# C spread over the partitions by transposes of its columns, and a new order of a chunk's work, in a Mamba and feed-forward block on one core

## The reference

```
xz = x W_xproj^T                 # 96 numbers per token: 64 rank, 16 B, 16 C
dt = softplus(rank W_dt^T + b)   # per token and channel
h  = exp(dt A) h + dt B x        # per channel and state, from token to token
y  = sum over states of h C, plus Dp x
x  = layernorm(x + y)
x  = layernorm(x + (silu(x Wg^T) * (x Wu^T)) Wd^T)
```

## Time and profile before

| | |
|---|---|
| median of 3 runs | 2120.16 us |
| the profiled execution | 2119.75 us |
| its span | 2118.0 us |
| busy: VectorE | 1985.9 us (94%) |
| busy: GpSimd | 1926.8 us (91%) |
| busy: TensorE, matmuls | 1558.5 us (74%) |
| busy: ScalarE | 1303.6 us (62%) |
| mean granted TensorE clock | 0.928 |

### The profile page before, as it was taken

One profiled execution on the slowest core, in us unless ns is written; L12 is line 12 of the kernel. 1 busy time (PEld: TensorE's weight loads), 2 busy tenths in 40 slices (PEclk: granted clock), 3 DMA queues, 4 the chain that ended last, 5 costly groups with the idle time before them and its releaser, 6 DMA issues.

```text
span 2118.0 us, 30230 instructions
## 1 busy us (share of the span) xinstructions
PE 1558.5 (74%) x8621; PEld 1140.7 (54%) x8744; DVE 1985.9 (94%) x2443; ACT 1303.6 (62%) x2157; POOL 1926.8 (91%) x877
## 2 busy tenths in 40 slices
PE   4677778777778777777777777777777877777775
PEld 1545555455555555555555555555555555555553
DVE  5799999999999999999999999999999999999982
ACT  4566666566666656666666666656666656666442
POOL 6999999999999999999999999999999999999950
PEclk6789999999999999999999999999999999999997
DMA  6332433223433322443322443422443422343200
GB/s 219 111 119 86 141 118 137 102 91 112 140 135 120 117 83 104 140 140 115 125 90 89 140 140 115 140 90 76 138 140 115 140 92 86 126 140 107 79 11 20
DMA packets 93455, 239.90 MB, mean 113 GB/s; under 512 B 8593, under 2 KB 42994, under 8 KB 77042
## 3 DMA queue, kind: packets, MB, share of 16 engines
q1 hardware_dynamic: 93426, 239.55, 32.5%
HBM read 220.65 MB, written 18.87 MB: 113 GB/s over the span
## 4 chain that ended last, share of the span: by engine, by line
issue 30%; POOL 28%; DVE 26%; PE 8%; ACT 6%; DVEq 2%; POOLq 1%; another core or an unknown queue 0%; ACTq 0%
POOL ub L388 16%; DVE h L620 10%; POOL h L398 8%; DVE h L629 6%; PE p_y L807 3%; DVE hid L665 2%; DVE silu_g L659 2%; ACT p_da L490 2%; DVE stats L635 2%; PE p_m L831 2%; DVEq L224 1%; PE p_o L842 1%; PE p_m L821 1%; POOL rstd L405 1%; DVE mean_var L639 1%
## 5 line engine op out<-in xcount | busy, mean ns | idle before, releaser
L388 POOL TENSOR_TENSOR ub<-u,b_bc 128x1024 f32<-128x1024 f32 x512 | 1203.9, 2372 | 0.1
L490 ACT ACTIVATE p_da<-dt,neg_a 128x512 f32<-128x512 f32 x1024 | 697.2, 687 | 426.1 <-DVE h L620 422.0
L620 DVE TENSOR_TENSOR_SCAN h<-p_da,h_carry,ub 128x512 f32<-128x512 f32 x512 | 641.5, 1271 | 2.2 <-ACT p_da L490 0.6
L398 POOL TENSOR_TENSOR h<-h,c_bc 128x1024 f32<-128x1024 f32 x256 | 606.8, 2371 | 33.5 <-ACT h_carry L485 32.8
L620 DVE TENSOR_TENSOR_SCAN h<-p_da,ub 128x512 f32<-128x512 f32 x512 | 610.1, 1212 | 8.1 <-ACT p_da L490 6.4
L807 PE MATMUL p_y<-ident,h 128*128 128x128 f32 x4096 | 572.2, 293 | 60.8 <-POOL h L398 59.6
L807 PEld LDWEIGHTS p_y<-ident,h 128*128 128x128 f32 x4096 | 518.8, 152 | 121.6 <-POOL h L398 81.9
L842 PE MATMUL p_o<-wt_down,hid 128*128 128x256 f32 x1536 | 353.7, 380 | 4.1 <-DVE hid L665 1.8
L842 PEld LDWEIGHTS p_o<-wt_down,hid 128*128 128x128 f32 x1536 | 287.6, 191 | 55.3 <-issue 13.9
L629 DVE TENSOR_TENSOR h<-h,p_c 128x1024 f32<-128x1024 f32 x256 | 306.1, 1196 | 9.8 <-PE p_c L792 5.2
L510 ACT ACTIVATE tanh_g<-p_m 128x512 f32<-128x512 f32 x192 | 114.7, 597 | 263.4 <-PE p_m L831 263.4
(11 more groups left out here) (72 smaller groups left out, 1289.3 us busy)
## 6 DMA issues: line engine op xcount, KB each, us to landing
b_bc<-bc_rows_dram SPq DMA_DIRECT2D x128, 1024.0 KB, 4.7
c_bc<-bc_rows_dram SPq DMA_DIRECT2D x256, 256.0 KB, 6.5
x_in<-in_L_attn_x SPq DMA_DIRECT2D x32, 512.0 KB, 7.2
out_x<-res_n SPq DMA_DIRECT2D x32, 512.0 KB, 3.3
bc_rows_dram<-bc_rows SPq DMA_DIRECT2D x32, 64.0 KB, 2.3
hid<-in_L_ffn_w_gate SPq DMA_DIRECT2D x1, 768.0 KB, 4.9
hid<-in_L_ffn_w_up SPq DMA_DIRECT2D x1, 768.0 KB, 6.7
res<-in_L_ffn_w_down SPq DMA_DIRECT2D x1, 384.0 KB, 7.1
```

Of the source, the lines that this page charges most:

```text
L388: nc.gpsimd.tensor_tensor(ub[:, s % UB_SLOTS, :, :], u[:, par, :, :], b_bc[:, s:s + 1, :].broadcast_to([P, DH, T]), ALU.mult).then_inc(s_u ...
L398: nc.gpsimd.tensor_tensor(h[:, s % H_SLOTS, :, :], h[:, s % H_SLOTS, :, :], c_bc[:, i:i + 1, :].broadcast_to([P, DH, T]), ALU.mult).then_i ...
L490: nc.scalar.activation(p_da[:, q, :], dt[:, par, q, :], ACT.Exp, scale=neg_a[:, q, s:s + 1]).then_inc(s_da, 1)
L620: nc.vector.tensor_tensor_scan(h[:, s % H_SLOTS, q, :], p_da[:, q, :], ub[:, s % UB_SLOTS, q, :], initial, ALU.mult, ALU.add).then_inc(s_s ...
```

## The change

C is no longer split in bfloat16 parts. The 32 rows of B and C of a chunk (`bc_rows`) are turned by four float32 transposes (`bc_turned`) into a free corner of `p_o`, copied to `bc_t` (`bc_cols`, one ScalarE copy of 128x128), and for each of VectorE's states TensorE takes column s of `bc_t`, repeats it 128 times as the operand of four transposes, and so fills `p_c`. The `rest`, `second_parts` and `third_part` jobs are gone, with `selector` and its four fillings on GpSimd. `project_dt` now waits for `rank_out` and `bc_out` alone. Four of GpSimd's states are others (6, 7, 8 and 10 to 12 with 1 and 2, where it had 4 and 8 to 12 with 1 and 2), and most entries of `AT` move.

```diff
-POOL_STATES = (1, 2, 4, 8, 9, 10, 11, 12)
+POOL_STATES = (1, 2, 6, 7, 8, 10, 11, 12)
...
-    "dt_of": (4, 2), "u_of": (9, 0),
+    "dt_of": (6, 2), "u_of": (11, 1),
...
+    "bc_turned": (6, 0), "bc_cols": (12, 1),
...
-            nc.scalar.copy(wt_proj[:, :, 0:R + BC], w_proj_t).then_inc(s_wt, 1)
-            nc.scalar.copy(wt_proj[:, :, SECOND], w_proj_t[:, :, FIRST]).then_inc(s_wt, 1)
+            nc.scalar.copy(wt_proj[:, :, :], w_proj_t).then_inc(s_wt, 1)
...
-                nc.scalar.copy(bc_rows[FIRST, :], p_m[FIRST, 0, :]).then_inc(s_rows, 1)
-                nc.scalar.copy(bc_parts[BOTH, par, :], p_m[BOTH, 0, :]).then_inc(s_part1, 1)
-
-            def second_parts(c, par):
-                wait(act, s_rest, c + 1)
-                nc.scalar.copy(bc_mid[FIRST, :], bc_rest[FIRST, :]).then_inc(s_part2, 1)
-                nc.scalar.copy(bc_parts[SECOND, par, :], bc_rest[SECOND, :]).then_inc(s_part2, 1)
+                wait(act, s_ones, 3)
+                wait(act, s_bt_ps, c)
+                nc.scalar.copy(bc_rows[ROWS, :], p_m[ROWS, 0, :]).then_inc(s_rows, 1)
+
+            def bc_cols(c, par):
+                act.wait_ge(s_bt_ps, c + 1)
+                wait(act, s_c_ps, ND * (c - 1))
+                nc.scalar.copy(bc_t[:, par, :, :], p_bc[:, :, ROWS]).then_inc(s_bt, 1)
...
-            def rest(c, par):
-                wait(dve, s_rank, c + 1)
-                wait(dve, s_part1, c + 1)
-                nc.vector.tensor_tensor(bc_rest[BOTH, :], p_m[BOTH, 0, :], bc_parts[BOTH, par, :],
-                                        ALU.subtract).then_inc(s_rest, 1)
-
-            def third_part(c, par):
-                wait(dve, s_part2, 2 * (c + 1))
-                nc.vector.tensor_tensor(bc_parts[THIRD, par, :], bc_rest[FIRST, :], bc_mid[FIRST, :],
-                                        ALU.subtract).then_inc(s_parts, 1)
...
             def project_dt(c):
-                wait(pe, s_rank, c + 1)
-                wait(pe, s_parts, c + 1)
+                pe.wait_ge(s_rank, c + 1)
+                pe.wait_ge(s_rows, c + 1)
...
             def broadcast_c(c, s, par):
                 i = DVE_STATES.index(s)
-                wait(pe, s_parts, c + 1)
+                pe.wait_ge(s_bt, c + 1)
                 wait(pe, s_hc_dve, ND * c + i)
-                nc.tensor.matmul(p_c[:, 0, :], selector[:, s, :], bc_parts[:, par, :],
-                                 start=True, stop=True).then_inc(s_c_ps, 1)
+                for k in range(TT):
+                    ins = nc.tensor.transpose(p_c[:, 0, k * P:(k + 1) * P],
+                                              bc_t[:, par, k, N + s:N + s + 1].broadcast_to([P, P]), ident[:, :])
+                ins.then_inc(s_c_ps, 1)
+
+            def bc_turned(c):
+                pe.wait_ge(s_rows, c + 1)
+                wait(pe, s_res, 2 * (c - 2))
+                for k in range(TT):
+                    ins = nc.tensor.transpose(p_bc[:, k, :], bc_rows[:, k * P:(k + 1) * P], ident[:, :])
+                ins.then_inc(s_bt_ps, 1)
```

More of the change, by code:

```diff
@@ L35 @@
     "weights": (7, 1),
-    "x_transposed": (0, 0), "x_out": (0, 1), "project": (1, 0), "rank_out": (1, 1), "bc_out": (1, 1), "rest": (2, 1),
-    "second_parts": (2, 0), "third_part": (2, 2), "project_dt": (2, 0), "softplus_abs": (4, 0), "softplus_exp": (4, 0), "softplus_log": (4, 0),
-    "dt_of": (4, 2), "u_of": (9, 0),
-    "z_out": (3, 0), "stats1": (3, 2), "mean1": (4, 0), "norm_inputs": (6, 1), "scalars": (7, 0), "norm1": (7, 0),
-    "x1_transposed": (8, 0), "x1_high": (8, 1), "x1_low": (9, 0),
-    "gate_up": (9, 2), "tanh": (9, 0), "silu": (10, 0), "hidden": (10, 1),
[3 rows of a table removed]
+    "x_transposed": (2, 0), "x_out": (2, 0), "project": (2, 2), "rank_out": (3, 1), "bc_out": (2, 1),
+    "project_dt": (4, 0), "softplus_abs": (5, 1), "softplus_exp": (5, 1), "softplus_log": (6, 0),
+    "dt_of": (6, 2), "u_of": (11, 1),
+    "z_out": (2, 0), "stats1": (2, 1), "mean1": (3, 2), "norm_inputs": (6, 0), "scalars": (6, 1), "norm1": (7, 0),
+    "x1_transposed": (8, 0), "x1_high": (8, 1), "x1_low": (10, 0),
+    "gate_up": (10, 0), "tanh": (10, 0), "silu": (10, 2), "hidden": (11, 0),
[3 rows of a table added]
+    "bc_turned": (6, 0), "bc_cols": (12, 1),
 }
@@ L304, in store @@
             def store(c):
-                wait(sp, s_out_ready, c + 2)
+                sp.wait_ge(s_out_ready, c + 2)
                 sp.dma_start(out_chunks[bass.ds(c, 1)].rearrange("a p k d -> (a p) k d"),
@@ L366, in _ @@
             nc.gpsimd.memset(ident[:, :], 0.0).then_inc(s_fill, 1)
-            nc.gpsimd.memset(selector[:, :, :], 0.0).then_inc(s_fill, 1)
             nc.gpsimd.memset(neg_half[:, :, :], -0.5)
-            pool.wait_ge(s_fill, 2)
+            pool.wait_ge(s_fill, 1)
             nc.gpsimd.affine_select(out=ident[:, :], in_=ident[:, :], compare_op=ALU.not_equal, fill=1.0,
                                     base=0, pattern=[[-1, P]], channel_multiplier=1).then_inc(s_const, 1)
[L373 to L377, removed]
             def u_of(c, par):
-                wait(pool, s_dt, c + 1)
+                pool.wait_ge(s_dt, c + 1)
                 nc.gpsimd.tensor_tensor(u[:, par, :, :], dt[:, par, :, :], x_t[:, par, :, :],
@@ L487, in decay @@
             def decay(c, s, par, q):
-                wait(act, s_dt, c + 1)
+                act.wait_ge(s_dt, c + 1)
                 wait(act, s_scan, 2 * units(c, s) - 2 + q - 1)
@@ L532, in _ @@
                 decay(0, 0, 0, q)
+            bc_cols(0, 0)
             act.wait_ge(s_const, 1)
@@ L607, in scan @@
             def scan(c, s, par, batch, q):
-                wait(dve, s_da, 2 * units(c, s) - 1 + q)
+                dve.wait_ge(s_da, 2 * units(c, s) - 1 + q)
                 if q == 0:
@@ L674, in residual @@
                     x1[:, 2 * a:2 * a + 2, :], ALU.mult, ALU.add).then_inc(s_res, 1)
-            rest(0, 0)
-            third_part(0, 0)
             dt_of(0, 0)
@@ L690, in step @@
                                     residual(c - 2, a)
-                        if nxt and due("rest"):
-                            rest(c + 1, 1 - par)
-                        if nxt and due("third_part"):
-                            third_part(c + 1, 1 - par)
                         if prev and due("stats1"):
@@ L760, in x_transposed @@
             def x_transposed(c):
-                wait(pe, s_x_in, 16 * (c + 1))
+                pe.wait_ge(s_x_in, 16 * (c + 1))
                 if isinstance(c, int) and c < 2:
@@ L774, in project @@
             def project(c, par):
-                wait(pe, s_xt, c + 1)
+                pe.wait_ge(s_xt, c + 1)
                 for q in range(DH):
-                    ins = nc.tensor.matmul(p_m[:, 0, :], wt_proj[:, q, :], x_t[:, par, q, :],
+                    ins = nc.tensor.matmul(p_m[0:R + BC, 0, :], wt_proj[:, q, :], x_t[:, par, q, :],
                                            start=(q == 0), stop=(q == DH - 1))
@@ L834, in gate_up, with down @@
                     ins.then_inc(done, 1)
-            def down(c, k, half):
+            def down(c, k, half, turned):
                 if k == 0 and half == 0:
-                    wait(pe, s_hid, NH * (c + 1))
+                    pe.wait_ge(s_hid, NH * (c + 1))
+                    wait(pe, s_bt, turned)
                 if k % 2 == 0 and half == 0:
@@ L851, in _ @@
             project_dt(0)
-            pe.wait_ge(s_const, 4)
+            bc_turned(0)
             pe.wait_ge(s_skip_diag, 2)
@@ L872, in step @@
                             project_dt(c + 1)
+                        if nxt and due("bc_turned"):
+                            bc_turned(c + 1)
                         if prev and due("x1_transposed"):
```

104 lines of the change are left out of this document (49 added, 55 removed), and 6 rows, old and new, of the table AT.

## The result

The changed kernel takes 2180.51 us, the median of 4 runs (2173.42 to 2186.74), against 2120.47 us for the kernel before. The ratio is 1.0284, with a 95% interval of 1.0268 to 1.0300. I had forecast 2060 us and a range up to 2100. The profiled execution has a span of 2184.4 us.

A forecast was written before the change was run, and what follows sets the result against it. VectorE's own list of work was taken as the bound: 2119.75 us less 52.7 (subtractions gone), 3.3 (earlier start) and 4 (shorter waits) is 2059.8, so 2060 us; range 2028 to 2100.

The forecast's parts named there:

- VectorE's own list of work sets the time: Whole kernel: VectorE's work is the bound, with some 3 us a pair of chunks lost to softplus and smaller waits.
- rival D: TensorE's chain: after idle stretches it runs at 1.2 GHz instead of 2.4, so the kernel is slower, 2150 us; chance 0.08.
- The rule of the Trainium skill: TensorE's transposes: they don't lift the clock and take about 275 ns each, 20 us on the kernel, 2080 us.
- The saving of 1.70 us a chunk: VectorE's scans: without the `rest` and `third_part` subtractions each chunk's list is 1.70 us shorter, 52.7 us over 31 chunks.
- The start: First chunk: the dt projection waits for the rows copy only, so it and the rest start 3.3 us earlier.
- The price of the new transposes: TensorE: 0.11 us for each transpose, also with a repeated column; 0.45 us for four.
- The chain through slots 2 to 8: Making dt later leaves small VectorE waits, some 0.8 us in odd and 1.5 in even chunks; 4 us gain kept.
- the forecast pass of 122.6: One loop pass, a pair of chunks: VectorE's pair falls from 126.28 us to near 122.6.
- GpSimd was no bound: GpSimd's 119.62 us of work a pair stays below VectorE's, so it keeps waiting at `norm_scalars`, less long.

The follow-up runs named there:

- the run with 24 fills: The changed kernel with 24 tiny fills of an unused tile on VectorE ahead of the loop: 2078.30 us, ratio 0.9805 to the kernel before.
- 267 to 600: The kernel before with 64 tiny fills on VectorE ahead of the loop, its loop body at these instruction numbers: 2158.15 us, ratio 1.0179.
- the run with 96 fills: The changed kernel with 96 tiny fills on VectorE ahead of the loop, its loop body at instructions 288 to 613: 2103.07 us, a single run.

## Why the prediction was wrong, point by point

- "VectorE's own list of work sets the time" failed as a sum of a list: it had no term for what happens between the end of a pass and the start of the next. That term is 102 us by the medians (2180.5 to 2078.3) and 107.7 by the two profiled executions; of the latter 68.0 is VectorE waiting for its instructions, and 31.6 are waits for `p_c`, `p_da` and tanh that vanish with it. Among the rivals there was none of this kind. It could be read beforehand only in part: the number of VectorE's instructions ahead of the loop and in it was known, and the page shows instruction queues, but no trace of before showed the stall, and no run measured what it would cost.
- The mechanism of rival D, TensorE's clock after an idle stretch, was at work, but the idle stretch came from the fetch: 12 products in 5.38 us against 2.85 without it. It did not come from transposes. In the run with 24 fills, which has all of them, a pass has a granted clock of 0.93 and VectorE waits 18.0 us in all for `p_c`, against 5.2 us in the kernel before, some 0.6 of it in each pass as forecast. The rule of the Trainium skill that I had weighed there, "TensorE: Matmul & The Clock Gate", section "Part 4: PE-mode transpose", found no support in that run: four transposes take 0.43 us from their start at 901.15 to the next start, not the 1.1 us that its 275 ns would give.
- The saving of 1.70 us a chunk fits; both subtractions left, and with the fetch gone the kernel is 42 us faster than the one before. No run measures it by itself. The start was right: the first `dt_of` begins at 23.27 us in the changed kernel and at 26.46 in the one before, 3.2 us earlier for a forecast of 3.3.
- The price of the new transposes was right: four in 0.43 us from start to start is 0.11 us each. The column repeated 128 times costs nothing more: four of the transposes of x take the same 0.60 us from first start to last end (949.65 in the changed kernel) as four for `p_c`.
- The chain through slots 2 to 8 was walked well. I had a late `p_c` for state 3 in even chunks (0.3 us; it is 0.64), a wait of the second residual (0.2 to 0.5; 0.18) and of the scans in slot 8 (0.5 to 1; 0.58). In the odd chunk of the same run, where I had 0.5 us for slot 8, six scans follow each other from 986.94 to 994.39 us without a wait. `dt_of` no longer waits in the loop, as forecast.
- The forecast without the fetch would still have been 18 us short. The missing term is `hidden` right behind the silu that it reads, 0.76 us where 0.58 is usual. In the run with 24 fills that is so in three of the six tiles: 3 x 0.18 x 32 = 17 us. Moving it out gave 18. The match is in part luck. From branch to branch the passes of that run have two lengths, 123.4 us (eight of 13) and 125.3 (five), the longer with about 1.5 us more of waits for tanh and `p_da`; with `hidden` moved, eight take 122.6 and five 123.2. So the passes without these waits shrank by 0.8 us, where the sum has 1.1, and the rest of the 18 came from the longer ones. The mean with `hidden` moved, 122.8 us, is close to the forecast pass of 122.6.
- GpSimd was no bound, as I said: 119.76 us busy in 123.99.

## What to carry to other kernels

When a loop's time grows and an engine idles at the first instruction of the body with no releaser, look at the packets of the instruction queues, and at the time from the engine's branch to its next instruction, before looking for a semaphore; a body that crosses one block more can cost a few microseconds a pass, and a few empty instructions ahead of the loop tell and cure it. Sum an engine's list from start to start, and give an instruction that reads what the one right before it wrote its own, longer step. Work taken off the bounding engine was won here only with the order changed as well: the transposes alone gave 8 us, none of it in the loop, with the new order and the loop mended 42, and with one job moved between two scans 60.

## What was not expected of the hardware

The stall at the jump back depends on where the body lies and not on its length alone. VectorE was late by 5.2 us in the mean for 192 to 517 (4.5 to 6.9), 2.4 us for 267 to 600 (1.5 to 3.2) and 1.2 us for 288 to 613 (0.9 to 1.7), each with some 80 packets in all. The traces show a good part of why. With the body at 192 there are two gaps in turn, 2.8 to 3.0 us ahead of its first instruction and 3.6 to 5.4 ahead of its second, so a border lies right behind the first; with the body at 288 there is the first gap alone, 2.8 to 3.0 us, and the second instruction follows in 0.1. VectorE's branch runs ahead of its work: at 905.70, in the run with 96 fills, work is left until 907.24, so that of the gap to 908.73 only 1.67 us show as idle time. With the body at 267 the one gap is 3.8 to 5.5 us; why it is longer stays open. The other instruction queue, q8, moved 15 packets in the changed kernel and 15 in the run with 24 fills, 0.25 MB, so 16 KB each: only the packets of 8 KB come again.
